# Running the LayerNorm products of a Mamba-and-experts layer behind four batches of expert matmuls instead of behind one

## The reference

```python
xn = layernorm(x)                                  # over the 1024 channels
# branch 1
p = xn @ in_proj_w.T; h, gate = p[..., :2048], silu(p[..., 2048:])
h = (grouped_causal_conv4(h) + conv_b) * gate      # 8 groups of 256 channels
hn = layernorm(h, ln_g, ln_b)                      # over the 2048 channels
h = silu(hn @ fc_w.T + fc_b) @ cproj_w.T + cproj_b + h
attn = h @ out_w.T
# branch 2: 8 experts, the best 2 of them per token, and a shared one
logits = xn @ Wr + expert_bias
top_v, top_i = top_k(logits, 2); rw = scatter(softmax(top_v), top_i)
moe = sum_e rw[:, e] * ((silu(xn @ Wg[e]) * (xn @ Wu[e])) @ Wd[e])
shared = (silu(xn @ Sg) * (xn @ Su)) @ Sd
y = x + attn + moe + shared
```

## Time and profile before

| | us |
|---|---|
| median of 3 runs shown | 7200.41 (6960.0 to 8038.26) |
| the profiled execution's own time | 6958.9 |
| its span, slowest core | 6957.4 (the eight cores: 6945.9 to 6957.4) |
| granted TensorE clock, mean | 0.966 to 0.968 on all cores |
| PE busy | 6428.1 (92%) |
| DVE busy | 2339.4 (34%) |
| ACT busy | 1859.5 (27%) |

### The profile page before, as it was taken

One profiled execution on the slowest core, in us unless ns is written; L12 is line 12 of the kernel. 1 busy time (PEld: TensorE's weight loads), 2 busy tenths in 40 slices (PEclk: granted clock), 3 DMA queues, 4 the chain that ended last, 5 costly groups with the idle time before them and its releaser, 6 DMA issues.

```text
span 6957.4 us, 83757 instructions; the slowest of 8 cores (6945.9 to 6957.4 us)
## 1 busy us (share of the span) xinstructions
PE 6428.1 (92%) x29600; PEld 2821.4 (41%) x29600; DVE 2339.4 (34%) x3858; ACT 1859.5 (27%) x2946; POOL 44.1 (1%) x85
## 2 busy tenths in 40 slices
PE   7878998989989899898999989899898998989988
PEld 2333443434434344343444434344343443434434
DVE  2233333423334232333333334333343333423234
ACT  3113223241232312323132232322314123231221
POOL 0000000000000000000000000000000000000000
PEclk9999999999999999999999999999999999999999
DMA  9995434444434444334443444343443434443433
GB/s 212 223 217 178 146 139 145 146 142 145 149 135 143 145 145 158 127 141 145 145 158 127 145 146 145 140 146 133 154 143 139 145 140 144 144 143 145 149 121 115
DMA packets 149779, 1035.17 MB, mean 149 GB/s; under 512 B 15488, under 2 KB 15488, under 8 KB 31872
## 3 DMA queue, kind: packets, MB, share of 16 engines
q1 hardware_dynamic: 133008, 939.62, 38.0%
q0 software_dynamic: 16368, 90.20, 6.8%
HBM read 996.22 MB, written 90.18 MB: 156 GB/s over the span
## 4 chain that ended last, share of the span: by engine, by line
PE 84%; DMA 7%; DVE 5%; issue 3%; ACT 1%; DVEq 0%; ACTq 0%; SPq 0%; POOL 0%; POOLq 0%
PE PS L221 81%; DMA ring<-wimg 4%; DMA wsc<-ring 3%; DVE tmp L547 2%; DVE tmp L553 1%; PE PS L425 1%; PE PS L431 1%; ACT xnf L380 0%; PE PS L771 0%; DVE xtok L857 0%; DVE scr L717 0%; PE PT L366 0%; PE PT L848 0%; DMA xtok<-x 0%; PE PS L709 0%
## 5 line engine op out<-in xcount | busy, mean ns | idle before, releaser
L221 PE MATMUL PS<-xnf,ring 128*128 128x512 bf16 x14336 | 3198.1, 385 | 303.3 <-ACT scr L574 260.4
L221 PEld LDWEIGHTS PS<-xnf,ring 128*128 128x128 bf16 x14336 | 1407.7, 99 | 2059.6 <-issue 446.0
L221 PE MATMUL PS<-scr,ring 128*128 128x512 bf16 x5120 | 1151.5, 384 | 24.5 <-DMA ring<-wimg 16.5
L737 DVE TENSOR_TENSOR yacc<-yacc,PS 128x512 f32<-128x512 f32 x1024 | 691.2, 686 | 1232.8 <-PE PS L221 1232.4
L221 PE MATMUL PS<-hpre,ring 128*128 128x512 bf16 x4096 | 927.2, 379 | 5.2 <-DMA ring<-wimg 5.0
L221 PEld LDWEIGHTS PS<-scr,ring 128*128 128x128 bf16 x5120 | 503.8, 99 | 647.2 <-issue 68.7
L221 PEld LDWEIGHTS PS<-hpre,ring 128*128 128x128 bf16 x4096 | 381.6, 97 | 531.2 <-issue 90.2
L756 ACT ACTIVATE scr<-PS 128x512 bf16<-128x512 f32 x384 | 229.3, 597 | 1144.8 <-PE PS L221 1096.3
L221 PE MATMUL PS<-tfc,ring 128*128 128x512 bf16 x2048 | 448.2, 381 | 8.6 <-DMA ring<-wimg 8.6
L221 PE MATMUL PS<-gate,ring 128*128 128x512 bf16 x2048 | 446.5, 380 | 7.5 <-DMA ring<-wimg 7.5
L672 DVE SCALAR_TENSOR_TENSOR gate<-PS,cvec_sb,hbuf 128x512 bf16<-128x512 f32 x256 | 192.2, 751 | 581.5 <-PE PS L221 581.5
(11 more groups left out here) (96 smaller groups left out, 2322.8 us busy)
## 6 DMA issues: line engine op xcount, KB each, us to landing
ring<-wsc SPq DMA_DIRECT2D x810, 1024.0 KB, 5.2
ring<-wimg POOLq DMA_DIRECT2D x54, 1024.0 KB, 32.3
wsc<-ring SPq DMA_DIRECT2D x54, 1024.0 KB, 25.5
xtok<-x SPq DMA_DIRECT2D x16, 2048.0 KB, 10.2
y<-xtok POOLq DMA_DIRECT2D x16, 2048.0 KB, 7.6
cvec_sb<-cvec SPq DMA_DIRECT2D x1, 40.0 KB, 1.9
wrsb<-wrimg POOLq DMA_DIRECT2D x1, 16.0 KB, 9.9
```

The costliest lines, as they stand in the source:

```text
L221: nc.tensor.matmul(PS[0:mh, lo:lo + TT], la, ra, start=st, stop=sp)),
L737: (lambda oc=oc, lo=lo: nc.vector.tensor_tensor(yacc[:, oc * TT:(oc + 1) * TT], yacc[:, oc * TT:(oc + 1) * TT], PS[:, lo:lo + TT], ALU.add)),
```

## The change

Only the order of the `p.add` calls of steps 3 to 6 changes; no operation is added, removed or resized. The order in the changed kernel is: the first half of the choice of experts with its Exp, `ln1_stats(i+1)`, `g0`, the two broadcasts, `u0`, `g1`, `u1`, the chain, the second half of the choice of experts, `fc`. The diff, with repeated bodies cut:

```diff
         # statistics end in abbf
-        for oc in range(4):            # g0, evicted by ACT with Silu
...
-        p.add("tensor", ... bcA)       # the two broadcasts
-        p.add("tensor", ... bcB)
-        for c in range(KI):            # the chain
...
-        for oc in range(4):            # u0, then g1, then u1
...
         p.add("vector", lambda: nc.vector.tensor_reduce(
             rsc[:, 0:4], rt3, AX.X, ALU.max),
...
         p.add("scalar", lambda: nc.scalar.activation(
             rsc[:, 12:16], rsc[:, 8:12], AF.Exp),
             reads=[R("rsc", 8, 12)], writes=[R("rsc", 12, 16)])
+        if i + 1 < n_tiles:
+            ln1_stats(i + 1)
+        for oc in range(4):            # g0
...
+        p.add("tensor", ... bcA)
+        p.add("tensor", ... bcB)
+        for oc in range(4):            # u0, then g1, then u1
...
+        for c in range(KI):            # the chain
+            s2 = c % 2
...
         p.add("vector", lambda: nc.vector.tensor_scalar_add(
             rsc[:, 16:20], rsc[:, 12:16], 1.0),
...
-        if i + 1 < n_tiles:
-            ln1_stats(i + 1)
```

More of the change, by code:

```diff
@@ L522, in build_nc @@
             reads=[R("rows", 0, 1024)], writes=[R("abbf", 512, 1024)])
-        for oc in range(4):
[L525 to L533, removed]
@@ L535, in build_nc @@
-        p.add("tensor", lambda: nc.tensor.matmul(
-            PS[:, 0:512], onesrow[0:1, :], abbf[0:1, 0:512], start=True, stop=True),
-            reads=[R("onesrow", 0, 128), R("abbf", 0, 512)],
-            writes=[R("PS", 0, 512)], tag="bcA")
-        p.add("tensor", lambda: nc.tensor.matmul(
-            PS[:, 512:1024], onesrow[0:1, :], abbf[0:1, 512:1024],
-            start=True, stop=True),
-            reads=[R("onesrow", 0, 128), R("abbf", 512, 1024)],
-            writes=[R("PS", 512, 1024)], tag="bcB")
@@ L544, in build_nc @@
-        for c in range(KI):
[L545 to L565, removed]
@@ L567, in build_nc @@
-        for oc in range(4):
-            if oc == 0:
-                load_slot(i, ("u", 0))
-            lo = next_bank()
-            mm_job(wslot(("u", 0), KD, 512, oc), xnf_rhs(), lo, tag=f"u0.{oc}")
-            dst, dreg = scr_reg(SG, oc)
-            p.add("scalar",
-                  (lambda dst=dst, lo=lo: nc.scalar.copy(dst, PS[:, lo:lo + TT])),
-                  reads=[R("PS", lo, lo + TT)], writes=[dreg])
-        for oc in range(4):
-            if oc == 0:
-                load_slot(i, ("g", 1))
-            lo = next_bank()
-            mm_job(wslot(("g", 1), KD, 512, oc), xnf_rhs(), lo, tag=f"g1.{oc}")
-            dst, dreg = scr_reg(HE0 + 2048, oc)
-            p.add("scalar",
-                  (lambda dst=dst, lo=lo: nc.scalar.activation(
-                      dst, PS[:, lo:lo + TT], AF.Silu)),
-                  reads=[R("PS", lo, lo + TT)], writes=[dreg])
@@ L586, in build_nc @@
-        for oc in range(4):
-            if oc == 0:
-                load_slot(i, ("u", 1))
-            lo = next_bank()
-            mm_job(wslot(("u", 1), KD, 512, oc), xnf_rhs(), lo, tag=f"u1.{oc}")
-            dst, dreg = scr_reg(UU, oc)
-            p.add("scalar",
-                  (lambda dst=dst, lo=lo: nc.scalar.copy(dst, PS[:, lo:lo + TT])),
-                  reads=[R("PS", lo, lo + TT)], writes=[dreg])
         rt3 = rtok[:, :].rearrange("p (s e) -> p s e", e=8)
@@ L624, in build_nc @@
             reads=[R("rsc", 8, 12)], writes=[R("rsc", 12, 16)])
+        if i + 1 < n_tiles:
+            ln1_stats(i + 1)
+        for oc in range(4):
+            if oc == 0:
+                load_slot(i, ("g", 0))
+            lo = next_bank()
+            mm_job(wslot(("g", 0), KD, 512, oc), xnf_rhs(), lo, tag=f"g0.{oc}")
+            dst, dreg = scr_reg(HE0, oc)
+            p.add("scalar",
+                  (lambda dst=dst, lo=lo: nc.scalar.activation(
+                      dst, PS[:, lo:lo + TT], AF.Silu)),
+                  reads=[R("PS", lo, lo + TT)], writes=[dreg])
@@ new lines, in build_nc @@
+        p.add("tensor", lambda: nc.tensor.matmul(
+            PS[:, 0:512], onesrow[0:1, :], abbf[0:1, 0:512], start=True, stop=True),
+            reads=[R("onesrow", 0, 128), R("abbf", 0, 512)],
+            writes=[R("PS", 0, 512)], tag="bcA")
+        p.add("tensor", lambda: nc.tensor.matmul(
+            PS[:, 512:1024], onesrow[0:1, :], abbf[0:1, 512:1024],
+            start=True, stop=True),
+            reads=[R("onesrow", 0, 128), R("abbf", 512, 1024)],
+            writes=[R("PS", 512, 1024)], tag="bcB")
@@ new lines, in build_nc @@
+        for oc in range(4):
+            if oc == 0:
+                load_slot(i, ("u", 0))
+            lo = next_bank()
+            mm_job(wslot(("u", 0), KD, 512, oc), xnf_rhs(), lo, tag=f"u0.{oc}")
+            dst, dreg = scr_reg(SG, oc)
+            p.add("scalar",
+                  (lambda dst=dst, lo=lo: nc.scalar.copy(dst, PS[:, lo:lo + TT])),
+                  reads=[R("PS", lo, lo + TT)], writes=[dreg])
+        for oc in range(4):
+            if oc == 0:
+                load_slot(i, ("g", 1))
+            lo = next_bank()
+            mm_job(wslot(("g", 1), KD, 512, oc), xnf_rhs(), lo, tag=f"g1.{oc}")
+            dst, dreg = scr_reg(HE0 + 2048, oc)
+            p.add("scalar",
+                  (lambda dst=dst, lo=lo: nc.scalar.activation(
+                      dst, PS[:, lo:lo + TT], AF.Silu)),
+                  reads=[R("PS", lo, lo + TT)], writes=[dreg])
@@ new lines, in build_nc @@
+        for oc in range(4):
+            if oc == 0:
+                load_slot(i, ("u", 1))
+            lo = next_bank()
+            mm_job(wslot(("u", 1), KD, 512, oc), xnf_rhs(), lo, tag=f"u1.{oc}")
+            dst, dreg = scr_reg(UU, oc)
+            p.add("scalar",
+                  (lambda dst=dst, lo=lo: nc.scalar.copy(dst, PS[:, lo:lo + TT])),
+                  reads=[R("PS", lo, lo + TT)], writes=[dreg])
+        for c in range(KI):
+            s2 = c % 2
+            p.add("vector",
+                  (lambda c=c, s2=s2: nc.vector.tensor_tensor(
+                      tmp[:, s2 * 512:(s2 + 1) * 512], hbuf[:, c * TT:(c + 1) * TT],
+                      PS[:, 0:512], ALU.mult)),
+                  reads=[R("hbuf", c * TT, (c + 1) * TT), R("PS", 0, 512)],
+                  writes=[R("tmp", s2 * 512, (s2 + 1) * 512)])
+            p.add("vector",
+                  (lambda s2=s2: nc.vector.tensor_tensor(
+                      tmp[:, s2 * 512:(s2 + 1) * 512],
+                      tmp[:, s2 * 512:(s2 + 1) * 512], PS[:, 512:1024], ALU.add)),
+                  reads=[R("tmp", s2 * 512, (s2 + 1) * 512), R("PS", 512, 1024)],
+                  writes=[R("tmp", s2 * 512, (s2 + 1) * 512)])
+            p.add("scalar",
+                  (lambda c=c, s2=s2: nc.scalar.activation(
+                      hpre[:, c * W + 3: c * W + 3 + TT],
+                      tmp[:, s2 * 512:(s2 + 1) * 512], AF.Identity,
+                      bias=cvec[:, 32 + c:33 + c], scale=cvec[:, 16 + c:17 + c])),
+                  reads=[R("tmp", s2 * 512, (s2 + 1) * 512),
+                         R("cvec_sb", 16 + c, 17 + c), R("cvec_sb", 32 + c, 33 + c)],
+                  writes=[R("hpre", c * W + 3, c * W + 3 + TT)])
```

## The result

The changed kernel takes 1.0233 times as long as the kernel before (95% interval 1.0208 to 1.0257). Those executions take 7120 to 7123 us against 6958 to 6960, which is 162 us more. I forecast 191 us more, 7150 us, with a range of 7088 to 7205. The 7120 us lie inside it, the median of all eight runs lies above it.

What follows compares the result with a forecast made beforehand. PE, busy 92% of the span, bounds the kernel, idling 260.4 us for u0's eviction. 14 middle tiles (174 us), the last (5) and tile 0 (12) add 191 to 6958.9: 7150 us, range 7088 to 7205.

Steps and rivals of the forecast that it cites:

- the clock: Lowered clock after idling, at u0 and after fc's first job: 2.1 and 1.9 us per middle tile.
- the hole in tile 0: DMA engines short of work in tile 0 because fc releases its ring slot late: about 12 us lost.
- the base: The profiled execution's own 6958.9 us, to which the forecast 191 us were added.
- First part: Expert choice's Exp and ln1_stats ahead of g0's eviction: first Silu 7.5 us later, u0 after 8.0 us of idling.
- rival D: As forecast, but a smaller delay before u0; 1 us per tile is 14 us; included in the forecast's 0.70.
- Second part: Chain behind u1's eviction: tmp's two halves hold DVE at chunk 2, PE loses 19.4 us at fc's first job.
- E: The end of u1's matmuls in a tile; fc's first job was forecast to end at about E + 22.85 us.
- rival C: DVE's half of the chain runs beside u0, g1 and u1, fc's first job 9.7 us earlier: 7004 us, chance 0.04.
- rival A: No clock loss at u0 or fc: 4.0 us less in each of 14 tiles, 7092 us, chance 0.12.
- the cover: In tile 0, most of PE's delay (fc some 40 us later) is made up where DMAs set the end.
- Rival B: Tile 0's delay is not covered: 28 us more, 7178 us, chance 0.12.
- The last tile: Tile without ln1_stats: first Silu 1.8 us late, chain behind u1 costs 3 us; together 5 us more.

Runs made afterwards that it cites:

- Only the chain moved: Changed kernel with the whole expert choice and ln1_stats put behind the chain, nothing new ahead of g0's evictions; 6989 to 6991 us.
- only the squares moved: Kernel before with the expert choice's first half and ln1_stats moved ahead of g0's evictions, chain left in place; lowest runs 7067.06 and 7068.45 us.
- The third experiment: Changed kernel, but DVE's second operation of a chunk writes bf16 into hpre instead of tmp, ACT working in place; cores took 6950 to 6979 us.
- The transposes: Changed kernel with 120 transposes of the identity added on PE between the broadcasts and u0; lowest run 7122.59 us.
- The early x: Changed kernel with the load of tile 1's x issued at program start; cores 4 and 5 took 7115.9 and 7114.9 us.

## Where the prediction was right, and the steps that failed

Both losses came where I had put them and by the mechanism that I had given. Three terms failed: the clock (1.9 us net per tile forecast, 0.8 measured, because I had put every place but two at no change), the hole in tile 0 (12 us forecast, nothing measured that stands out of the differences between cores), and the base, for which I took the profiled execution alone.

**First part, squares ahead of g0's eviction: right.** I had 7.5 us more before `u0`; it is 7.47 (8.34 less 0.87), so rival D's smaller first part did not come either. "Only the chain moved" takes them away and "only the squares moved" brings them alone.

**Second part, the chain behind u1: right, 0.5 us too long.** The last `hpre` operation let PE's matmul 15 start 22.24 us after E (1564.68, where the next matmul would have started without a wait, to 1586.92); I had 22.43. Counting that matmul's slow run both in the job and in what follows it made up most of the rest. Without the clock the tile is 9.98 us longer (75.84 against 65.86, the first three stages less their losses of clock), where I had 10.5. The third experiment shows the held buffer, and rival C fell with it.

**The clock: the places right, the term too large.** I took 2.1 us at `u0` and 1.9 at `fc` for the 2.07 at `g1` that goes, 1.9 net. Measured are 1.83 (24.36 against 22.53 where nothing idles) and 1.6 (113 matmuls in 26.04 us, at the full clock 24.4). So rival A, no cost of the clock in the two new places, is out. But two other places changed as well, which I had not counted at all. Behind the earlier trace rows the 64 matmuls of expert 2 took 1.1 us more than before (16.56 and 15.46). And at the tile's end, at the transposes of `ln1_apply` (L366) with their short waits, the clock fell in the kernel before and mostly does not in the changed one. One tile of each, before first:

```profile
1384.00:1386.00 2.00, 1.86 (x13) 1.15 (x12) 0.00 (x0) 1.72 (x3) 0.00 (x0) 0.50 0.14 57
1386.00:1388.00 2.00, 2.00 (x6) 0.72 (x5) 0.00 (x0) 0.49 (x1) 0.00 (x0) 0.50 0.04 8
```

```profile
1412.00:1414.00 2.00, 1.45 (x18) 0.95 (x16) 0.00 (x0) 1.72 (x3) 0.00 (x0) 1.00 0.15 61
1414.00:1416.00 2.00, 2.00 (x11) 0.91 (x10) 0.69 (x1) 1.00 (x1) 0.00 (x0) 1.00 0.04 8
```

The stage with this place took 283.3 us or more in 10 of before's 14 tiles on core 1, and 280.9 in 13 of the changed kernel's 14. Against 280.9 the means are 1.8 and 0.1 us over, so 1.7 us came back there. All in all the clock costs 0.8 us more per tile than before, not 1.9. Core 1 is the extreme here: the long stage stands in 4 to 10 tiles by core, and from the mean of all eight cores before to that of cores 0 to 3 after the two places changed by 0.9 and -1.25 us instead of 1.1 and -1.7.

The two places hang together. In the kernel before, on core 1, the three tiles whose expert 2 took 16.4 to 16.8 us ended with a stage of 280.9 us, and the ten that ended with 283.3 us or more had taken 15.1 to 15.3 us at expert 2: the clock fell at one of the two places and not at both. In the changed kernel it fell behind the earlier trace rows in all 14 tiles of core 1 (16.5 to 16.8 us), and in one of them at the tile's end as well.

The step that failed is the assumption that the other places with short gaps keep their clock loss when the program around them is shifted. The transposes show it from the other side: most of one fall taken away came back elsewhere. What decides whether such a gap makes the clock fall was not settled by these runs; the gaps at L366 are the same in both kernels up to the fall (1.67, 0.1 and 0.5 us), only their times have moved.

**Tile 0: the cover right, the hole too dear.** I had 12 us with bounds of 0 and 40. PE waited 35.95 us for Silu, as forecast. The DMA engines' share by stretch on core 1:

```profile
216.00:225.00 9.00, 3.65 (x7) 0.73 (x7) 8.27 (x14) 5.28 (x7) 0.00 (x0) 0.50 0.99 236
225.00:234.00 9.00, 7.39 (x23) 2.61 (x23) 2.39 (x9) 2.85 (x4) 0.03 (x1) 0.64 0.45 188
234.00:240.00 6.00, 6.00 (x30) 2.68 (x28) 0.00 (x0) 0.84 (x2) 0.50 (x1) 1.00 0.67 126
240.00:250.00 10.00, 10.00 (x48) 4.47 (x47) 0.00 (x0) 2.06 (x3) 1.06 (x2) 1.00 0.79 139
```

The hole came at 225, where I had it from 220 on, with some 9 us of missing share (0.55 of 9, 0.33 of 6, 0.21 of 10). But from tile 0's broadcast to tile 1's it took 3.8 us more on core 1 (513.54 and 509.74) and 3.7 less on core 0 (505.72 and 509.45); over cores 0 to 3 the mean is 509.5 against 508.6. So it costs nothing that stands out of the differences between cores. The early x, with which the DMA share in these stretches is 0.99 to 1.05, agrees: its cores 4 and 5 take 510 us for this piece. The step that failed is charging the hole to the end of the tile in full; why it cost so little no run shows. Rival B (28 us more) is out.

**The last tile: right.** 5 us forecast, 6.0 measured on core 1 and 4.5 to 5.8 on cores 0, 2 and 3.

**The base: the lowest execution, not the median one.** I added the sum to the 6958.9 us of the profiled execution, at the low end of the runs shown, and put what lifts other runs above it at nothing. So the 7150 us and the range up to 7205 can be held only against executions like that one; the median of all eight runs, 7279.3 us, lies 74 us above the range. The changed order is not what lifts it: the median of the kernel before is 7320.23 us.

**The sum:** of the 29 us between 191 and 162 on core 1, 23 are the middle tiles (14 times 1.65: 1.1 clock, 0.5 chain) and 7 tile 0 (12 forecast, 5.3 measured, of which 1.5 came before the first broadcast), less 1 in the last. The chances named slower by over 2% at 0.84; it came at 2.3%, nearer to the 2% line than the forecast's 2.7%.

## What to carry to other kernels

On an engine that evicts results and also does other work, count for every operation what stands between it and the evictions that the matmuls wait for. Moving a block whole from ahead of the evictions to behind them moves the wait to the block's reader; spread between the evictions, the same block with the same two buffers left PE 0.5 us of waiting per tile instead of 16. And before a producer is expected to run ahead, count its buffers: with two halves it is never more than two chunks ahead of the reader, wherever its own instructions stand.

## What the runs showed of the hardware that I had not expected

The granted clock does not fall at the same gaps in every tile of one kernel, nor in two kernels that have the same gaps: at L366's transposes 10 of 14 tiles of core 1 lost 2.4 us in the kernel before and hardly one in the changed kernel, and where it did not fall there it had mostly fallen behind expert 2's start. Closing one gap of 8 us with 120 transposes kept the clock at 1.00 there and saved 1.83 us, of which 0.2 to 0.8 us per tile remained in all. And ACT's operation with gain and bias took 0.80 us from a bf16 source in SBUF, against 0.82 from float32, although its squares from bf16 take 0.63. In these rows the length goes with the number of vector operands of an operation on 128 by 512 and not with the type of its source: 0.57 to 0.63 with none (casts, Silu of `g1`, the squares of `h`), 0.69 with `fc`'s bias (L655), 0.80 to 0.82 with gain and bias.
